# A transposed activation gets a PSUM bank of its own, one step later, and GpSimd computes one inverse root earlier

## The reference

```python
x = x + tanh(g_xattn) * attention(layernorm(x), ctx, ctx)   # 32 query heads, 8 key/value heads of 16
x = x + tanh(g_ffn)  * ffn(layernorm(x), ...)
# ffn: probs = softmax(x @ Wr); top 4 of 32 experts, at most 64 tokens an expert;
#      shared = silu(x @ Wsg) * (x @ Wsu) @ Wsd * sigmoid(x @ Wse); experts of width 352
```

## Time and profile before

| | us |
|---|---|
| median of three runs | 2347.98 |
| the profiled execution | 2348.52 |
| its span in the profile | 2346.6 |
| attention stage | about 0 to 755 |
| FFN stage | about 756 to the end |
| granted TensorE clock, mean of the span | 0.996 |

### The profile page before, as it was taken

The page is one execution under the profiler, slowest core; times in us unless marked ns, Lnnn a source line. Parts: engine busy times, 40 slices in busy tenths (PEclk is TensorE's granted clock), DMA queues, the critical chain, the costliest instruction groups (busy, mean ns, idle before and its releaser), DMA issues.

```text
span 2346.6 us, 40408 instructions
## 1 busy us (share of the span) xinstructions
PE 2285.5 (97%) x12289; PEld 1754.2 (75%) x12289; DVE 1152.6 (49%) x2284; ACT 762.5 (32%) x1184; POOL 722.3 (31%) x1459
## 2 busy tenths in 40 slices
PE   6999999999997999999999999999999999999999
PEld 5767666766675887777777777777777777777777
DVE  5899899999996842232323322223232232323232
ACT  5888888888885110110101101010010110101010
POOL 6888888888883200000000000000000000000100
PEclk9999999999998999999999999999999999999999
DMA  2555555555554322223221232212322222222411
GB/s 73 144 143 136 144 134 140 139 140 134 143 136 135 64 92 98 69 96 103 83 78 63 81 118 83 78 63 78 106 87 84 67 78 90 90 84 86 139 68 43
DMA packets 276366, 235.12 MB, mean 100 GB/s; under 512 B 129505, under 2 KB 203233, under 8 KB 276322
## 3 DMA queue, kind: packets, MB, share of 16 engines
q1 hardware_dynamic: 271970, 221.89, 31.5%
q0 software_dynamic: 4352, 12.65, 1.9%
HBM read 161.88 MB, written 71.57 MB: 99 GB/s over the span
## 4 chain that ended last, share of the span: by engine, by line
PE 66%; DVE 1%; DMA 0%; issue 0%; DVEq 0%; POOLq 0%
PE acc L1125 7%; PE p_u L1141 7%; PE p_u L1143 7%; PE p_u L1142 7%; PE acc L1127 7%; PE acc L1126 7%; PE p_g L1141 7%; PE p_g L1143 7%; PE p_g L1142 7%; PE p_x L1173 2%; PE p_y L1160 2%; PE p_x L1160 2%; PE p_x L1151 0%; PE p_y L1166 0%; DMA rows<-out_dram 0%; DVE rows L1105 0%
## 5 line engine op out<-in xcount | busy, mean ns | idle before, releaser
L1059 DVE TENSOR_TENSOR act_f<-p_u,act_f 128x512 f32<-128x512 f32 x176 | 121.7, 692 | 984.4 <-PE p_u L1143 984.3
L964 ACT ACTIVATE act_f<-p_g 128x512 f32<-128x512 f32 x176 | 105.3, 598 | 1215.6 <-PE p_g L1143 1194.8
L565 DVE TENSOR_REDUCE negmax<-p_max 128x8 fp32r<-128x1024 f32 x256 | 312.5, 1221 | 55.0 <-PE p_max L710 50.6
L451 ACT ACTIVATE probs<-p_exp 128x1024 f32<-128x1024 f32 x256 | 262.2, 1024 | 60.1 <-PE p_exp L669 60.1
L1125 PE MATMUL acc<-wd_h,hh 128*128 128x512 f32 x704 | 279.9, 398 | 0.0
L1141 PE MATMUL p_u<-xh,wgu_h 128*128 128x512 f32 x704 | 274.5, 390 | 3.8 <-DVE act_f L1059 3.8
L1141 PE MATMUL p_g<-xh,wgu_h 128*128 128x512 f32 x704 | 276.0, 392 | 0.0
L1126 PE MATMUL acc<-wd_l,hh 128*128 128x512 f32 x704 | 274.7, 390 | 0.0
L1127 PE MATMUL acc<-wd_h,hl 128*128 128x512 f32 x704 | 274.7, 390 | 0.0
L1143 PE MATMUL p_g<-xh,wgu_l 128*128 128x512 f32 x704 | 274.4, 390 | 0.0
L1142 PE MATMUL p_g<-xl,wgu_h 128*128 128x512 f32 x704 | 274.4, 390 | 0.0
(11 more groups left out here) (142 smaller groups left out, 3703.1 us busy)
## 6 DMA issues: line engine op xcount, KB each, us to landing
ew<-in_L_ffn_Wg_dram SPq DMA_DIRECT2D x32, 704.0 KB, 5.9
ew<-in_L_ffn_Wu_dram SPq DMA_DIRECT2D x32, 704.0 KB, 8.2
xs<-in_x_dram SPq DMA_DIRECT2D x64, 256.0 KB, 2.7
xres<-in_x_dram SPq DMA_DIRECT2D x64, 256.0 KB, 2.9
out_dram<-x SPq DMA_DIRECT2D x64, 256.0 KB, 2.7
xn_rows<-xn SPq DMA_DIRECT2D x64, 256.0 KB, 3.1
xn_cols<-xnT SPq DMA_DIRECT2D x64, 256.0 KB, 3.4
rows<-out_dram SPq DMA_DIRECT2D x16, 1024.0 KB, 5.2
```

The costliest lines, as they stand in the source:

```text
L451: nc.scalar.activation(probs[c][:, :], p_exp[:, :, :].rearrange("p a b -> p (a b)"), ACT.Exp, scale=float(D) ** -0.5).then_inc(exp_done, 1)
L565: nc.vector.tensor_reduce(negmax[c // 2][:, 0:16].rearrange("p (g c i) -> p c i g", g=2, c=2)[:, c % 2, :, :].bitcast(F32R), p_max[:, :, : ...
```

## The change

Four things are changed.

- A PSUM bank p_xn is added; the transposes of xn of batch B-3 write into it instead of p_pv. TensorE issues them at c = 2, after the router matmuls of B-4, instead of at c = 1 before o_cols. Their wait for `pv_done` goes, and so does the wait of pv's first half for `xnT_done`.
- ScalarE copies xnT (L458) at c = 3, after the exponential and ahead of the two copies of the keys, instead of at c = 1.
- SyncE issues the store of xnT at the end of its list for the iteration, ahead of the weight pieces, instead of at c = 1.
- GpSimd runs inverse_root of B-2 directly after inverse_root of B+2 and before norm_x of B+2.

```diff
             p_ot = ps("p_ot", [128, 512])
+            p_xn = ps("p_xn", [128, 512])
...
-                            if (B - 3).ok:
-                                b = B - 3
-                                wait(sp, xnT_done, b.n + 1)
-                                alone(sp, spare_s)
-                                sp.dma_start(xT_dram[:, :, bass.ts(b.n, 128)].rearrange("k p t -> p k t"), xnT[b.par][:, :, :]).then_inc(xnT_out[b.par], 16)
                         if c == 2 and (B + 3).ok:
                             load_in(B + 3)
                         if c == 2 and (B - 2).ok:
                             b = B - 2
                             wait(sp, x2_done, b.n + 1)
                             sp.dma_start(out_rows[bass.ts(b.n, 128), :], x2[b.par][:, :]).then_inc(x2_out[b.par], 16)
+                    if (B - 3).ok:
+                        b = B - 3
+                        wait(sp, xnT_done, b.n + 1)
+                        alone(sp, spare_s)
+                        sp.dma_start(xT_dram[:, :, bass.ts(b.n, 128)].rearrange("k p t -> p k t"), xnT[b.par][:, :, :]).then_inc(xnT_out[b.par], 16)
                     if weights_load(B):
...
                         inverse_root(B + 2, stat1, mv1, ve1, rs1, qraw_done, rs1_done)
-                        norm_x(B + 2)
                     if (B - 2).ok:
                         inverse_root(B - 2, stat2, mv2, ve2, rs2, xn_done, rs2_done)
+                    if (B + 2).ok:
+                        norm_x(B + 2)
...
-                        if c == 1 and (B - 3).ok:
+                        if c == 3 and (B - 3).ok:
                             b = B - 3
                             act.wait_ge(xnT_mm, b.n + 1)
                             wait(act, xnT_out[b.par], 16 * b.half)
                             wait(act, lg_mm, b.n - 1)
-                            nc.scalar.activation(xnT[b.par][:, :, :].rearrange("p k t -> p (k t)"), p_pv[:, :], ACT.Copy).then_inc(xnT_done, 1)
+                            nc.scalar.activation(xnT[b.par][:, :, :].rearrange("p k t -> p (k t)"), p_xn[:, :], ACT.Copy).then_inc(xnT_done, 1)
...
-                    if s == 0 and (b - 2).ok:
-                        pe.wait_ge(xnT_done, b.n - 1)
...
-                        if c == 1 and (B - 3).ok:
-
-                            b = B - 3
-                            pe.wait_ge(xn_done, b.n + 1)
-                            pe.wait_ge(pv_done, 2 * b.n + (4 if (b + 1).ok else 2))
-                            wait(pe, xnT_done, b.n)
-                            for k in range(KC):
-                                last = tr(p_pv[:, 128 * k:128 * k + 128], xn[b.par][:, 128 * k:128 * k + 128], ident[:, :])
-                            last.then_inc(xnT_mm, 1)
...
                             last.then_inc(lg_mm, 1)
+                        if c == 2 and (B - 3).ok:
+
+                            b = B - 3
+                            pe.wait_ge(xn_done, b.n + 1)
+                            wait(pe, xnT_done, b.n)
+                            for k in range(KC):
+                                last = tr(p_xn[:, 128 * k:128 * k + 128], xn[b.par][:, 128 * k:128 * k + 128], ident[:, :])
+                            last.then_inc(xnT_mm, 1)
```

## The result

The changed kernel takes 2387.92 us (median of four, 2387.49 to 2389.41) against 2347.88 us before (2347.57 to 2348.48): ratio 1.0171, 95% interval 1.0154 to 1.0189. It is 40 us slower. The forecast was slower by 16 us, range to 2384; the sign held, the size did not.

The account below looks back on a forecast made before the run. GpSimd's own operations set the pace, beside a TensorE-VectorE loop of 11.175 us a batch. The terms made 11.46, +0.285 us over 60 batches, less 1.2: +16 us on the median 2348.0, so 2364 us, range 2346 to 2384.

Parts of the forecast that it names:

- The loop as the thing to sum: TensorE's p_max groups and the VectorE reductions emptying their banks: 11.175 us a batch before, 11.46 forecast.
- P1 to P2: Start of a batch's second p_max group to its third, TensorE's own queue: 3.40 us, forecast 3.86.
- P3 to P1: Start of a batch's fourth p_max group to the next batch's second: 5.56 us, forecast 5.35.
- GpSimd's reordering takes away the wait for the root: VectorE's 0.40 us wait ahead of xn goes; GpSimd's stream falls from 11.175 to 10.93 us.
- N3 to N0: VectorE's last p_max reduction to the next batch's first: 3.44 us, forecast 3.04 in plain batches; 3.37 in weight batches.
- Transposes, +0.46 us: Four transposes on TensorE, moved behind the second p_max group, lengthen P1 to P2 to 3.86 us.
- The copy on ScalarE, +0.60 us on P3 to pv: xnT copy ahead of k_evac delays pv after the fourth p_max group, 1.22 to 1.82 us; called the largest term.
- Weight batches: Batches with GpSimd's weight piece: 11.46 us if xn keeps 0.55 us, 11.60 if 0.97; 11.46 taken.
- the third rival: VectorE's xn held behind GpSimd's weight piece: +0.68 us in every second batch, 2384 us, chance 0.17.
- SyncE: "I take 0": Moved xnT store ahead of the weight loads delays the row of maxima by 0; upper bound 0.4 us every second batch.
- End of the stage, -1.2 us: Last router matmuls of the attention stage: with the router group first, about 1.2 us saved once.
- The port: GpSimd and VectorE share an exclusive lock, first comer keeps it; taken for every operation, an estimate above 2390 us.

Follow-up runs that it names:

- pool_only: The kernel before with GpSimd's reordering alone (second root ahead of norm_x): 2347.8 us, ratio 0.9993.
- tr_store: The changed kernel with the transposes back at c = 1 and the store of xnT one iteration later: 2351.3 us, ratio 1.0012.
- w_mid: The changed kernel with GpSimd's weight piece between k_stacks and q_stacks of the next iteration: 2367.9 us, ratio 1.0081.
- store_next: The changed kernel with the store of xnT issued at c = 1 of the next iteration: 2378.4 us, ratio 1.012.
- no_swap: The changed kernel with GpSimd's old order (norm_x ahead of the second root), the other moves kept: 2382.6 us, ratio 1.0141.
- tr_back2: The changed kernel with the transposes back at c = 1 ahead of o_cols, still in their own bank, run again: 2369.9 us, ratio 1.0094.
- copy_late: The changed kernel with ScalarE's copy of xnT behind the key copies and the next query copy: 2491.2 us, ratio 1.0606.
- slack_place: The changed kernel with the weight piece between the stacks, store and copy at c = 1, transposes at c = 1 directly before p_max: 2335.8 us, ratio 0.9946.

## Why the prediction was wrong

The direction, the loop and most terms held; the forecast failed on two steps that it set at nothing.

- **The loop as the thing to sum**: right. P1 to P2, P2 to P3 and P3 to P1 add up to the mean batch in every row of the table.
- **GpSimd's reordering takes away the wait for the root**: right (27 waits to none over the same 640 us); VectorE's own N3 to N0 was put at 3.04 us and is 3.06 in pool_only. GpSimd does fall from pacemaker to waiting for statistics (55 waits).
- **Transposes, +0.46 us**: right, 0.43 (tr_store, and 3.84 against 3.41).
- **The copy on ScalarE, +0.60 us on P3 to pv**: the mechanism right, the size too large: 1.22 became 1.70 in plain batches and 1.61 in weight ones, because the next copy starts 0.48 us after L460 (409.00 to 409.48), not after its whole 0.60. But P0 to N0 is 0.86, not 0.76 us, where VectorE comes from other work, so P3 to P1 came out as forecast, 5.34 against 5.35. "The largest term" was wrong all the same: taken away by itself it gives back 6 us (2378.4 to 2372.1), the transposes 27 (2378.4 to 2351.3). The forecast's own sum had it so: against VectorE's own queue the copy adds 3.99 - 3.80 = 0.19 us to a batch, the transposes 0.46.
- **Weight batches: "I take 11.46, because the weight piece is now issued after norm_x, about when xn ends"**: this step failed. It holds for xn, and the third rival, which had xn blocked, is refuted too: xn took 0.62 us. What starts when xn ends is is_top, and it took the blow: 3.67 us from N3 to N0 where w_mid has 3.12, 5.78 instead of 5.24 from P3 to P1. The rival's place was right and its price near (0.68 us in every second batch and 2384 us, against 0.54 measured), its victim was not. Moved away, the piece gives back 20 us.
- **SyncE: "I take 0"**: this step failed, and the room was not the wrong part. In medians over the batches with weight loads, the first load's issue comes 1.16 us after P3 before and 0.73 in store_next, so the work ahead of it does come 0.43 us earlier relative to P3. But the added store puts the first load at 1.39: 0.66 us for one more issue, not 0.55. The 0.15 us that counted as free before the row was not free: the row follows the end of the second load's issue by at least 0.11 us in every batch, before and after, and 0.11 to 0.13 when the queue decides; before, queue and maxima let it go at the same time. And the second load's issue itself takes 0.77 us instead of 0.49. So the row comes 2.78 us after P3 instead of 2.26.

  TensorE feels it only in part, 4.12 against 3.84 us from P1 to P2, inside the bound of 0.4 in every second batch. The three batches whose second load took 0.51 to 0.53 us kept P1 to P2 at 3.84 to 3.85, and the longest, 0.94 us, went with 4.27. So the loss followed an issue whose length the prediction took as fixed. Why it gets longer stays open: it takes 0.71 to 0.77 us in after, no_swap, w_mid and tr_back2, 0.47 to 0.52 in the other runs, copy_late among them, where the store also stands ahead of the loads. Moved away, the store gives back 9.5 us.
- The store's wait for its copy is not what delays the row here. SyncE's own list of waits over 100 to 740 us has one in every second batch only:

```profile
SPq L50 <- ACT xnT L460: 11.1, 27, 0.9
```

  Where the weight loads follow, the store comes 0.65 us behind the store of x2 (409.17 to 409.82), about as the first load did before (414.29 to 414.91). In copy_late the copy does decide.
- The two together give 25, less than 29.5: in w_mid the wait for the row had already shrunk a little (4.05 against 4.12, some 2 us); the rest is within the intervals.
- **End of the stage, -1.2 us**: wrong in sign. From the last p_max to the key transposes it is 793.26 - 765.97 = 27.3 us after and 756.01 - 729.39 = 26.6 before. A part of the saving came: from the router group behind the last wait for a row to the last router group it is 787.55 - 774.50 = 13.05 us, and 750.33 - 736.53 = 13.80 before. More was lost ahead of it, where TensorE waits longer for the row and then runs at a granted clock of 0.50 for 3 us (1.00 in the same place before): 3.01 us from that p_exp to its router group, 1.66 before. After, then before:

```profile
771.49 1.22 PE L669 MATMUL p_exp<-qt,kt 128*128 128x512 f32 x2 [1.82 <-DMA qt<-maxT]
772.64 1.94 PE L644 MATMUL p_pv<-probs,vals 128*32 128x512 f32 x8
```

```profile
734.87 0.73 PE L669 MATMUL p_exp<-qt,kt 128*128 128x512 f32 x2 [0.96 <-DMA qt<-maxT]
```

- **The port**: the Trainium skill, SBUF — State Buffer, section "Who interferes with whom", also says that a VectorE instruction with two SBUF inputs contends with a GpSimd instruction that reads SBUF. By that rule, the trace agrees: is_top has two inputs and ended at 401.72, 0.14 us after L414 (401.58). The other half of the rule that the prediction takes from this section of the Trainium skill, that whoever comes first keeps the pair for its whole instruction, the traces bear out only in part: in slack_place xn and is_top run to their end inside a norm_x that began 1.3 us before xn (see the end), and there the measurement decides. I had read the section for casts and tensor_scalar and had not asked which neighbour of xn has two inputs. The fear that the small cast ahead of xn would block beside norm_x did not come true: its 64 instances took 155 to 172 ns.

## What to carry to other kernels

When four engines are nearly full, write down the loop as starts of the same few groups (here p_max and its reduction), put each moved operation on a segment, and price it there: the same four transposes cost nothing before P1 and 0.43 us behind it. A moved operation must be followed through every queue that it stands in: behind an issue that waits for a copy, all later issues wait too (copy_late), and the length of an issue is not fixed (0.49 us became 0.77). And an operation of GpSimd that slides in time has to be held against each two-input neighbour on VectorE, not only against the one it used to meet.

## What the runs showed of the hardware

- A VectorE comparison of 128x128 with two SBUF inputs takes 0.37 us beside GpSimd's small tensor_scalar operations and 1.02 us beside a tensor_tensor of 128x352; it ends 0.14 us after it. It goes both ways: in slack_place VectorE's residual took 1.23 us instead of 0.75, begun while GpSimd's tensor_tensor L372 ran, and GpSimd's four-column copy, 0.18 us otherwise, took 0.66 beside the residual.

```profile
404.90 1.23 DVE L547 SCALAR_TENSOR_TENSOR x<-o_sb,tanh_x,xres 128x512 f32<-128x512 f32 x1
...
405.52 0.66 POOL L379 COPY top<-v 128x4 f32 x1
```

- The operation that starts first does not always hold up the other to its own end. In slack_place xn starts 1.3 us into GpSimd's norm_x in nearly all plain batches, takes 0.54 us (0.55 in the kernel before) and ends 0.46 us before norm_x does; is_top follows inside norm_x too, in 0.28 us, and norm_x takes 2.32 us instead of 2.09. In nearly all weight batches xn starts 1.4 us or more into norm_x, takes 0.93 us and ends 0.27 us after it. Spans on GpSimd are rough, and what divides the two cases is not shown. One of the plain ones:

```profile
409.73 2.33 POOL L340 TENSOR_SCALAR qraw<-xs,mv,rs 128x512 f32<-128x512 f32 x1
...
411.06 0.54 DVE L516 TENSOR_SCALAR xn<-x,mv,rs 128x512 f32<-128x512 f32 x1
```

- After TensorE had stood still for 1.58 us in copy_late, its granted clock was 0.55 for the next 6 us, near the lower of its two levels (1.2 of 2.4 GHz), and pv took 1.93 us instead of 1.06. The waits of 0.2 to 0.6 us in the changed kernel show no such loss (granted 1.00 over its 640 us). The stretch of copy_late, columns as in the earlier trace rows:

```profile
412.20:418.20 6.00, 5.96 (x27) 3.91 (x27) 1.77 (x5) 1.62 (x2) 2.57 (x9) 0.55 0.57 166
```

The loss did not follow every such wait. All 22 plain batches of copy_late between 100 and 700 us have the row equally late; in nine of them P1 to P2 took 5.7 us, in the others 7.15 to 8.45. Over the 3 us from the late p_exp the granted clock was 1.00 in each of the nine and 0.50 to 0.68 in each of the others. The nine are the wait alone (at 174.74, after 1.59 us of waiting, pv took 1.07 us); where the clock fell it cost a further 1.5 to 2.7 us. What decides between the two is not shown.
